# Six extra matmuls on constants behind each tile of the row passes of a four-layer graph network

## The reference

```python
edge_index = jnp.stack([src, dst])
h = relu(layernorm(x)); x = x + L0(h)   # three relation-weighted sums, then attention over all edges
h = relu(layernorm(x)); x = x + L1(h)   # graph attention, 8 heads of 16
h = relu(layernorm(x)); x = x + L2(h)   # mean of neighbours and edge features
h = relu(layernorm(x)); x = x + L3(h)   # sum over edges of one of two linear maps, by edge type

# one of the three sums of L0 (edges are heads <- tails):
msg = rel_w[rels][:, None] * h[tails]
agg = jax.ops.segment_sum(msg, heads, num_segments=N_ENT) + h
return jnp.tanh(agg @ W)
# L2
msg = x_nei[src] + edge_attr @ w_edge_W.T
out = jax.ops.segment_sum(msg, dst, num_segments=n)
# L3
msg = jnp.where((edge_types == 0)[:, None], m_data, m_ctrl)
agg = jax.ops.segment_sum(msg, dst, num_segments=X.shape[0])
```

## Time and profile before

| | us |
|---|---|
| median of 3 runs | 10414.67 |
| lowest and highest | 10411.96, 10428.05 |
| the profiled execution | 10415.44 |
| its span, first to last instruction | 10413.7 |
| mean granted clock of TensorE | 0.614 of full speed |

### The profile page before, as it was taken

One profiled execution on the slowest core, in us unless ns is written; L12 is line 12 of the kernel. 1 busy time (PEld: TensorE's weight loads), 2 busy tenths in 40 slices (PEclk: granted clock), 3 DMA queues, 4 the chain that ended last, 5 costly groups with the idle time before them and its releaser, 6 DMA issues. The chain is left out here.

```text
span 10413.7 us, 108515 instructions
## 1 busy us (share of the span) xinstructions
PE 5831.4 (56%) x17424; PEld 3587.3 (34%) x17424; DVE 5604.8 (54%) x20814; ACT 1045.8 (10%) x3382; POOL 6484.6 (62%) x6595
## 2 busy tenths in 40 slices
PE   0577046666556565656566664777754444564444
PEld 0455022223333333333233333555533333333333
DVE  7566057776455444555666776666673333423333
ACT  0000000000000000000333332333320000010000
POOL 3777766666666656665566654666646666446665
PEclk9655566767666676667666665555555555555555
DMA  2233111112111121112111121111111111111112
GB/s 40 63 81 91 11 35 46 46 46 54 46 46 47 46 54 46 47 46 53 42 43 43 44 40 44 45 45 45 45 35 56 43 43 44 39 53 46 46 46 54
DMA packets 397376, 491.62 MB, mean 47 GB/s; under 512 B 135602, under 2 KB 302070, under 8 KB 396438
## 3 DMA queue, kind: packets, MB, share of 16 engines
q0 software_dynamic: 208736, 381.82, 15.3%
q1 hardware_dynamic: 184938, 101.44, 3.4%
q10 hardware_dynamic: 3020, 1.36, 0.1%
HBM read 448.60 MB, written 37.86 MB: 47 GB/s over the span
## 5 line engine op out<-in xcount | busy, mean ns | idle before, releaser
L1173 PE MATMUL PS<-OH,RING 128*128 128x128 f32 (+1 forms) x9816 | 3661.3, 511 | 2892.0 <-issue 932.3
L1173 PEld LDWEIGHTS PS<-OH,RING 128*128 128x128 f32 x9816 | 2231.3, 279 | 4321.6 <-issue 1810.0
L1677 POOL DMA_INDIRECT RING<-TAB,IDX x2418 | 2316.6, 958 | 1225.9 <-issue 629.4
L601 DVE TENSOR_TENSOR RA<-RA,PS 128x256 f32 x2418 | 1008.9, 417 | 1426.4 <-PE PS L1173 608.3
L601 DVE TENSOR_TENSOR RB<-RB,PS 128x128 f32 x2490 | 719.0, 289 | 1347.6 <-PE PS L1173 710.1
L1677 POOL DMA_INDIRECT RING<-TABM,IDX x830 | 786.2, 947 | 545.1 <-issue 183.7
L1693 POOL DMA_INDIRECT RING<-TABQ,IDX x806 | 783.6, 972 | 535.4 <-PE PS L1259 265.3
L1656 POOL DMA_INDIRECT REC<-RC x800 | 953.3, 1192 | 252.7 <-issue 242.8
L1677 POOL DMA_INDIRECT RING<-TABN,IDX x830 | 786.8, 948 | 509.0 <-PE PS L1173 246.5
L589 DVE TENSOR_SCALAR OH<-IOTA,KEY,WE 128x256 f32<-128x256 f32 x2418 | 1024.1, 424 | 87.9 <-ACT RA L1473 45.7
L1259 PE MATMUL PS<-OH,RING 128*128 128x256 f32 x1612 | 756.0, 600 | 394.4 <-ACT OH L1497 240.4
(11 more groups left out here) (361 smaller groups left out, 5336.6 us busy)
## 6 DMA issues: line engine op xcount, KB each, us to landing
RING<-in_edge_attr_dram SPq DMA_DIRECT2D x830, 64.0 KB
RING<-TAB,IDX POOLq DMA_INDIRECT x2418
RING<-TABN,IDX POOLq DMA_INDIRECT x830
RING<-TABM,IDX POOLq DMA_INDIRECT x830
RING<-TABQ,IDX POOLq DMA_INDIRECT x806
REC<-RC POOLq DMA_INDIRECT x800
TAB<-HN SPq DMA_DIRECT2D x18, 512.0 KB, 3.2
RING<-TABG,IDX POOLq DMA_INDIRECT x560
```

The lines of the kernel that those rows point to most:

```text
L601: v.tensor_tensor(sl, sl, PS[k % 4][:, 0:width], ALU.add).then_inc(s_ad, 1)
L1173: t_.matmul(PS[t % 4][:, 0:width], GD[:, t % 16, :], OH[:, t % 4, 0:width], start=True, stop=True).then_inc(s_mm, 1)
L1677: p.indirect_dma_start(GD[:, t % 16, :], None, table, bass.IndirectOffsetOnAxis(ap=idx[:, t:t + 1], axis=0)).then_inc(s_ring[t % 16], 16)
```

## The change

Behind the tile's matmul, in all row passes but ATTR, TensorE runs six matmuls of IDENTB (as weights, 128x128, bfloat16) with IOTAB (256 columns, bfloat16) into the first 256 columns of PS[7]. They wait for nothing, raise no semaphore, and nothing reads what they write. TensorE runs its instructions in order, so the waits and the matmul of tile t + 1 stand behind the six of tile t; s_mm of tile t is raised by the tile's own matmul, ahead of them. The other engines' instructions are the same, in the same order.

```diff
                     if t >= 4:
                         t_.wait_ge(s_ad, base + t - 3)
                     t_.matmul(PS[t % 4][:, 0:width], GD[:, t % 16, :], OH[:, t % 4, 0:width], start=True, stop=True).then_inc(s_mm, 1)
+                    if i != ATTR:
+                        for _ in range(6):
+                            t_.matmul(PS[7][:, 0:256], IDENTB[:, :], IOTAB[:, :], start=True, stop=True)
```

## The result

| | kernel before | with the six matmuls |
|---|---|---|
| median of 3 runs, us | 10414.67 | 10584.35 |
| lowest and highest | 10411.96, 10428.05 | 10573.58, 10596.53 |
| span of the profiled execution | 10413.7 | 10582.5 |
| mean granted clock | 0.614 | 0.803 |

The change makes the kernel slower by 170 us: the ratio is 1.016, its 95% interval 1.0147 to 1.0174. The forecast had the sign right and the size wrong: it said +385 us.

What follows compares the result with a forecast made beforehand. It took the gather's 1.25 us per tile plus stalls between VectorE and TensorE as the bound. Half of 775 us of longer burst steps, about +390, on 10415.44 gave 10,805, less 0.77 for the median: 10,800 us; range 10,050 to 12,500.

Steps and rivals of the forecast that it cites:

- The bound: In the five changed passes: no engine is the limit; gathers every 1.25 us set a floor of 5097 us, stalls add 860.
- slow stretch: Part of a pass between bursts of quick additions: steps of 3.5 us, where extra matmuls were costed at nothing.
- The row that says it: In MEAN: a wait of 10.17 us, cited as not a matmul's length and against the faster rival.
- The lengths: TensorE's need per tile with the six: 2.13 us low, 1.07 high for wide tiles; 1.71 and 0.86 for narrow.
- In a burst they don't fit: In stretches of quick additions: steps grow from 0.65 to at least 1.07 us (wide), about 0.5 to 0.86 (narrow); 775 us.
- The second sum: At the start of about 240 bursts: two to four wide tiles at the lower clock, each 0.9 us late, 430 to 860 us.
- The first sum: Longer burst steps over the five passes: 181, 84 (SUM0), 191, 194 and 125 us, together 775 if nothing is given back.
- Each extra matmul pays: Rival, in the slow stretch: delay is paid per instruction, +900 to 4500 us, over 12,500 us in all; chance 0.07.
- TensorE becomes the bound: Rival, in the five passes: at the lower clock TensorE needs 7989 us in place of 5957.8, giving 12,450; chance 0.13.
- Faster: the slow stretches end: Rival, in the five passes: busier TensorE keeps the upper clock, gathers set the pace, 760 us less, 9,655; chance 0.20.
- No change: Rival, in the five passes: all six lie in TensorE's idle time, 10,400 to 10,436 us; chance 0.12.

Runs made afterwards that it cites:

- e11: The kernel before, without the gathers of tiles 16 and later in the five passes: 7,558 us, ratio 0.7247 to the kernel before (10,432 us there).
- e12: The kernel with the six matmuls, without the gathers of tiles 16 and later in the five passes: 8,731 us, ratio 0.8373 to the kernel before (10,432 us there).
- e1: Twelve extra matmuls of 256 columns per tile in place of six: 11,487 us, ratio 1.092 to the kernel before (10,524 us there).
- e2: Six extra matmuls per tile of 16 columns in place of 256: 10,745 us, ratio 1.0217 to the kernel before (10,524 us there).
- e10: Three extra matmuls of 512 columns per tile in place of six of 256: ratio 1.0054 to the kernel before (10,432 us there).
- e14: Six extra matmuls per tile of 16 columns in place of 256: ratio 1.0008 to the kernel before (9,123 us there).
- e15: Twelve satisfied waits of TensorE per tile in place of the six matmuls: ratio 1.0013 to the kernel before (9,123 us there).
- e18: 24 satisfied waits of TensorE per tile in place of the six matmuls: ratio 1.0986 to the kernel before (9,116 us there).
- e3: The kernel before, with GpSimd waiting for the addition of tile t - 16 instead of its matmul: 10,500 us, ratio 0.998 (10,524 us before there).

## Why the prediction was wrong in size

**The bound.** Right that no engine's own work is the bound and that 1.25 us per gather is the floor. On P chips that floor is reached. Left open there was what makes a step in the slow stretch 3.5 us long. It is that TensorE's reports come late while gathers run (e11 against the kernel before, same chip); what makes them late stays open. The row that says it stood among mine as a mere oddity. TensorE beside it, in the kernel before:

```profile
8309.52 0.79 PE L1168 MATMUL PS<-ROWS,ONES 1*128 1x128 f32 x2
8321.63 0.58 PE L1173 MATMUL PS<-OH,RING 128*128 128x128 f32 x1 [11.31 <-DVE OH L592]
```

TensorE was through at 8310.3, VectorE went on at 8320.71, 10.4 us later, and TensorE did nothing in between.

**The lengths.** Right: 1.07 to 1.09 us for a wide tile (e12, 1.09), 0.86 to 0.88 for a narrow one (e12, 0.88 for most of TYPED's spacings), 1.74 with twelve (e1). The clock went to 0.98 in SUM0+1, where I had asked for over 0.8. TensorE's busy time came to 963 us, a little under the 1000 that I named.

**The step that failed** is "In a burst they don't fit", with its sum of 775 us of which I took half, 390. It rests on the belief that additions follow TensorE's pace. They don't on an L chip: VectorE works off several reports at once, and its quick additions are 0.65 us apart with the six as without. The additions over 3 us apart in SUM0+1 even fell from 105 to 28, while those over 1.3 us rose from 282 (the prediction says 285; from start to start it is 282) to 333. What grew is GpSimd's idle time, by 40 us in that pass. In place of +0.1 us per tile the runs show +0.04 (174 us over 4078 tiles), and it isn't made of columns alone (e2, e10). Why the six make the cycle of late reports longer on L chips, no run shows. The second sum, 430 to 860 us for tiles at the lower clock, fell away: the clock was 0.98 in the wide passes and 0.88 and 0.91 in the narrow ones. The first sum has a slip of its own as well: SUM0's 84 us doesn't come out of the trace, since its 558 short spacings average 1.045 us, 0.045 us less than 1.09, which makes 25 us. And that the forecast had slower right is partly luck: the same change costs nothing on a P chip.

**MEAN** lost least, 12.7 us, because its further terms gained. Idle time ahead of VectorE's L569, before and after:

```profile
L569 DVE TENSOR_SCALAR HN<-PS,RDEG 128x128 f32<-128x128 f32 x49 | 17.2, 351 | 485.6 <-remote 474.9 <-PE PS L1168 6.4 <-issue 4.4
```

```profile
L569 DVE TENSOR_SCALAR HN<-PS,RDEG 128x128 f32<-128x128 f32 x49 | 17.2, 351 | 198.8 <-remote 112.2 <-PE PS L1168 73.7 <-issue 12.9
```

9.9 us for each of the 49 became 4.1. Part of either is the wait for TensorE to come to these matmuls (2.9 us in e12, where no report is late). Counted from the end of L1168's record to the start of L569, the 49 average 9.3 us before and 1.8 us after. So these reports came through sooner with the six, a gain that my sum didn't have. Why, no run shows.

**The rivals.** "Each extra matmul pays" may have had the right kind of cost, which e2 and e10 point to and don't prove, at a price five to 26 times too high: 170 us, not 900 to 4500. "TensorE becomes the bound" happens only with twelve, and at the full clock, not the lower level (e1). "Faster: the slow stretches end" is what P chips look like, but not by the clock: e14 and e15 reach 1.25 us per tile with 0.77 and 0.62 of the clock in SUM0+1, and the kernel before takes the same time there. "No change" is the answer on the P chips: there the gather's 1.25 us, my floor, covers all of it. The rule of the Trainium skill (Perfetto Trace Analysis, "Matmul Optimizations"), that matmuls should run back to back since the engine scales with use, is borne out for the clock, 0.67 to 0.98, and brought no time here, since the matmul is not what ends last. It doesn't hold by busy share alone: e18 has TensorE busy 959 of 1160 us in SUM0+1 at 0.50.

## What to carry to other kernels

Matmuls that only keep TensorE busy are free at most as far as something else covers their length, here the gather's 1.25 us per tile; without it they cost 1.09 - 0.65 us per tile. Even under that cover they cost 1.6% where reports were late. Where they are wanted, try a few long ones before many short ones: at equal columns three of 512 cost a third of six of 256, in one comparison on one L chip. And before a stall is charged to an engine, compare the end of its record with the moment at which the next engine moves: a gap of several us with nothing running belongs to neither, and it may be there on one chip and not on the next.

## What the runs showed of the hardware

- On L chips s_mm rises 1.8 to 3.6 us after the matmul's record ends while gathers run (3104.26 and 3107.13 for records that end at 3102.47 and 3103.56), and then several times at once; the reports of MEAN's further matmuls took 9.3 us on average and up to 12.4 in the kernel before. Without gathers, on the same chip, or with gathers 1.74 us apart (e1, SUM0+1), they are prompt, as on P chips. What holds them up is not known: neither who waits on the semaphore (e3) nor the clock (e2 has late reports at 0.68, the change at 0.98).
- The same kernel took 10,415 to 10,524 us on chips of one kind and 9,116 to 9,133 on three of the other, some 14 to 15% apart. A change's worth can differ in the same way: +1.6% in both comparisons on L chips, nothing on a P chip.
- TensorE's clock was at its upper level of 2.4 GHz through whole passes with gaps of 1.5 us in its work every five tiles (0.98 in SUM0+1), and at the lower level of 1.2 GHz where it was busy 959 of 1160 us with matmuls and waits in turn (e18, 0.50).
- 24 satisfied waits made TensorE's tile about 0.58 us longer (e18, 1.43 us against 0.85).
